# Layer 3's stages beside the next group: four engines on one shared pace, and the same stages with a place of their own for each engine

## The chip, the cores and the metric

One core of a Trainium2 chip runs the whole program. Its engines are TensorE (PE in the profile, with PEld for the loading of weights), VectorE (DVE), ScalarE (ACT), GpSimd (POOL) and SyncE (SP, which here only issues transfers). Each runs its own instructions strictly in the order in which the program gives them, and waits at semaphores for the others. The metric is the device time of one execution in microseconds; lower is better.

## What is computed

Four layers in a row over a batch of 64 sequences of 64 tokens with 256 features, all in float32. Layers 0 to 2 are attentions of x over a context; layer 2 ends in an MLP of 1024 hidden units. Layer 3 is a recurrent block:

```
Mo = softmax(Mn^T Mm) applied to Ml;  x = Wo Mo + x                  # layer 0, channel attention
x = layernorm(gqa(x, ctx) + x)                                       # layer 1, 32 heads of 8
h = rmsnorm(attention(x over [ctx, x]) + x); x = mlp(h) + x          # layer 2, 16 heads of 16
xa = ln(x); sx = shift(xa) - xa                                      # layer 3
xxx = einsum(tanh((xa + sx * maa_x) @ maa_w1), maa_w2)
xk, xw, xv, xr, xg = xa + sx * (maa_stack + xxx)
w = exp(-exp(decay + tanh(xw @ td_w1) @ td_w2)); r, k, v, g = products of xr, xk, xv, silu(xg)
s = k v + w s, over time; out = r (u k v + s)                        # the scan
x1 = x + (groupnorm(out) * g) @ Wo.T
y = x1 + sigmoid(xr2 @ Wfr.T) * (relu(xk2 @ Wfk.T) ** 2 @ Wfv.T)     # xk2, xr2: ln(x1), shifted and mixed
```

## The kernel before

The batch goes in eight groups of eight sequences. `group_block(now, before, after)` is one block of instructions for all engines: it computes layers 0 to 2 of group `now`, layer 3 of group `before`, and near its end loads group `after`. It is called for group 0 (without a layer 3), six times in a loop and once more with both, and at last with a layer 3 alone. So seven blocks hold both kinds of work; they are called turns here. Blocks don't overlap: all engines meet between two of them.

In a turn, layers 0 to 2 are a software pipeline written out by hand. Each engine runs `for i in range(END)` with END = 61. In iteration i layer 0 has its units at i = 0 to 10; layer 1 has its 16 units of scores at i = 14 to 29 (A1 = 14), and layer 2 its 16 at i = 35 to 50 (A2 = 35), each unit going through PE (scores), DVE (`masked`, `largest`), POOL (`subtract`), ACT (`exps`), PE (`turned`) and ACT again. `pair`, `divide`, `project` and `add` follow once for four units; the last `project` of layer 2 (L888) is at i = 58, and what it gives is squared, normalised and turned (`xnT`) by i = 60. Behind the loop PE has the 8 products "u" of the MLP, each with `gelu` on ACT, and two products "y2".

Layer 3 of the group before is a list of stages in order, `STAGES`: 18 from "moments" to "bonus", 19 stages of scans, and 11 from "center" to "ffn v". Every engine calls `layer3(stage)` with its own part of each. In scan stage n POOL makes the products of state n + 1, DVE runs the scan n over time (L1185) and reads the one before (L1197), and PE adds read n - 3 into a bank with one product (L658). When they are called is set by steps: `step()` counts and runs what is due at that count. There are 4 steps ahead of the loop, one in each iteration, one behind each "u" and each "y2", and `rest()` runs what is left.

```python
PACE = {"r u k": 2.2, "shift": 2.2, "maa": 2.2, "gate": 2.4, "shift 2": 2.2,
        "mix 4": 1.0, "r": 1.0, "v": 1.0, "decay": 1.0, "td": 1.2}
due, at = {}, 0.0
for stage in STAGES:
    due.setdefault(int(at), []).append(stage)
    at += PACE.get(stage, 1.0 if stage[0] == "scan" else 1.6)
```

So all engines have a stage in the same iteration: "maa" at i = 3, "mix 0" at 5, "mix 1" at 6, "td" 8, "k" 9, "mix 2" 11, "decay" 12, "v" 13, "mix 3" 14, "mix 4" 16, "r" 17, "g" 18, "r u k" 20, "bonus" 22, the scans one in each iteration from 23 to 41, "center" 42, "variance" 44, "gate" 46, "project" 48, "moments 2" 50, "normalize 2" 51, "turn 2" 53, "shift 2" 54, "ffn k" 57, "ffn r" 58, "ffn v" 60. Nothing of layer 3 is beside the MLP's "u" and "y2". Products of layer 3 go through two banks of their own (ring "late"), those of the other layers through six others.

In an iteration the step comes first on PE, ACT and POOL; on DVE it comes behind `layer0`, `masked` and `largest` and ahead of `normalized`, `divide` and `add`. DVE's `normalize_ahead` for the next group comes behind the "u" steps, and waits for ACT's `deviations_ahead`, which also comes there. SP stores the result of layer 3 (L570) once "ffn v" is done, and waits until it has landed before the block can end. `tables(...)` loads a table of functions on ACT (L928) when another one is set.

## Time and profile before

| | |
|---|---|
| median of 3 runs | 2241.07 us |
| the runs | 2231.89, 2241.07, 2241.25 us |
| the profiled execution, its own time | 2240.95 us |
| its span, first to last instruction | 2239.2 us |
| PE busy | 1800.2 us, 80% |
| DVE busy | 1363.9 us, 61% |
| ACT, POOL busy | 849.3 and 860.1 us, 38% each |
| mean granted clock of TensorE | 0.907 of full speed |
| first "mm" of group 0 (layers 0 to 2 alone) | at 42.4 us |
| the seven turns | from 224.3 to 2092.3 us |
| layer 3 of the last group, alone | from 2092.3 us to the end |

Busy is time in which an engine has an instruction in work. A granted clock of 1.00 is 2.4 GHz, 0.50 is 1.2 GHz; a value between is a stretch with both. Where an engine sat idle, the profile names what ended the idle time. In float32 one matmul of the program shows as two instructions of PE.

### The profile page before, as it was taken

To read this page: it belongs to the slowest core of one execution; us is meant where nothing else is said; L and a number is where in the kernel's file an instruction comes from. 1 tells how busy PE (TensorE), PEld (TensorE's weight loads), DVE (VectorE), ACT (ScalarE), POOL (GpSimd) and SP (SyncE) were. 2 spreads that over 40 slices of the span, in tenths; PEclk is the share of its full clock that TensorE was granted. 3 is DMA by queue.
4 is the path that set the end of the run, shared out by engine and by line. 5 is a ranking of instruction groups with operands and counts; after the bars stand their busy time and mean duration, and the time that the engine had idled before them with its cause. 6 is when DMAs were issued, how large, how long until landed. Compare 5 with 4: busy or idle time off the path is not lost. (4 is left out here: it accounts for less than half of the span.)

```text
span 2239.2 us, 37086 instructions
## 1 busy us (share of the span) xinstructions
PE 1800.2 (80%) x13613; PEld 1098.1 (49%) x13613; DVE 1363.9 (61%) x2332; ACT 849.3 (38%) x1680; POOL 860.1 (38%) x905
## 2 busy tenths in 40 slices
PE   3888887888788787887888878788887888788765
PEld 2565444654356444554445634465444654456413
DVE  3652568635886368753687446873578645875283
ACT  1443432533425333353333533253432543425202
POOL 3531257302672037511384114830257303752060
PEclk9999998999899898898988989899988999889967
DMA  5000011010210102010020101201011010200030
GB/s 157 1 1 25 7 39 39 2 41 1 48 30 13 29 1 63 15 35 7 15 63 1 34 8 25 53 2 41 1 39 39 2 39 1 63 15 11 1 77 10
DMA packets 73611, 61.24 MB, mean 27 GB/s; under 512 B 38960, under 2 KB 56512, under 8 KB 73408
## 3 DMA queue, kind: packets, MB, share of 16 engines
q1 hardware_dynamic: 49600, 41.70, 8.9%
q10 hardware_dynamic: 23264, 16.85, 2.6%
q8 instruction: 122, 2.00, 0.4%
q14 instruction: 81, 0.66, 0.1%
q0 software_dynamic: 544, 0.03, 0.0%
HBM read 20.28 MB, written 4.19 MB: 11 GB/s over the span
## 5 line engine op out<-in xcount | busy, mean ns | idle before, releaser
L1508 POOL TENSOR_TENSOR soft_ring<-soft_ring,seg_max 128x512 f32<-128x512 f32 x256 | 324.2, 1274 | 471.7 <-DVE seg_max L1349 470.9
L1056 ACT ACTIVATE soft_ring<-soft_ring 128x512 f32<-128x512 f32 x256 | 160.8, 628 | 399.3 <-POOL soft_ring L1508 391.6
L658 PE MATMUL bank<-late,pick 128*128 128x512 f32 x256 | 176.4, 779 | 97.4 <-DVE late L1197 97.1
L1343 DVE SCALAR_TENSOR_TENSOR soft_ring<-bank,mask 128x512 f32<-128x512 f32 x256 | 164.4, 683 | 108.2 <-PE bank L716 100.4
L1470 POOL TENSOR_TENSOR late<-late 128x520 f32<-128x520 f32 x128 | 188.7, 1474 | 64.8 <-DMA late<-late 50.1
L1185 DVE TENSOR_TENSOR_SCAN late<-late 128x520 f32<-128x520 f32 x128 | 188.3, 1471 | 19.2 <-POOL late L1472 13.7
L857 PEld LDWEIGHTS bank<-ident,soft_ring 128*128 128x128 f32 x1024 | 126.5, 151 | 122.8 <-issue 97.8
L857 PE MATMUL bank<-ident,soft_ring 128*128 128x128 f32 x1024 | 170.0, 298 | 19.8 <-ACTq L1067 14.0
L1516 POOL TENSOR_SCALAR soft_ring<-soft_ring,rden 128x256 f32<-128x256 f32 x64 | 59.1, 924 | 312.4 <-DVE rden L1310 312.4
L716 PE MATMUL bank<-early 64*128 64x512 f32 (+1 forms) x512 | 128.2, 603 | 58.6 <-ACTq L1049 55.2
L1349 DVE TENSOR_REDUCE seg_max<-soft_ring 128x8 f32<-128x512 f32 (+1 forms) x256 | 169.3, 676 | 8.9 <-DVE early L1406 1.9
L581 PE MATMUL bank<-late,maa 128*128 128x512 f32 (+1 forms) x224 | 127.3, 686 | 23.4 <-DVEq L1177 19.3
L928 ACT ACT_TABLE_LOAD x55 | 70.6, 1283 | 157.2 <-issue 100.8
L1197 DVE TENSOR_TENSOR late<-late 128x512 f32<-128x512 f32 x128 | 122.9, 960 | 0.3 <-PE bank L658 0.3
L658 PEld LDWEIGHTS bank<-late,pick 128*128 128x128 f32 x256 | 50.3, 233 | 143.8 <-DVE late L1197 99.6
L581 PE MATMUL bank<-early,w 128*128 128x512 f32 x256 | 114.7, 607 | 7.4 <-ACT early L1104 7.4
L913 PE MATMUL bank<-w,early 128*128 128x256 f32 x512 | 111.8, 379 | 0.0
L716 PEld LDWEIGHTS bank<-early 64*128 64x128 f32 x512 | 50.3, 218 | 118.8 <-issue 117.2
L913 PEld LDWEIGHTS bank<-w,early 128*128 128x128 f32 x512 | 97.3, 190 | 16.6 <-issue 3.8
L943 ACT ACTIVATE early<-bank,vec 128x512 f32<-128x512 f32 x96 | 66.0, 687 | 102.9 <-PE bank L581 99.8
L1046 ACT ACTIVATE soft_ring<-bank,nmax 128x256 f32<-128x256 f32 x128 | 59.4, 469 | 113.5 <-DVE nmax L1306 109.7
L943 ACT ACTIVATE late<-bank 128x512 f32<-128x512 f32 (+2 forms) x104 | 61.8, 594 | 99.7 <-PE bank L581 97.8
(242 smaller groups left out, 3430.1 us busy)
## 6 DMA issues: line engine op xcount, KB each, us to landing
late<-late SPq DMA_DIRECT2D x128, 260.0 KB, 3.0
c<-in_ctx ACTq DMA_DIRECT2D x8, 512.0 KB, 4.3
x<-in_x ACTq DMA_DIRECT2D x8, 512.0 KB, 5.9
out_x<-late SPq DMA_DIRECT2D x8, 512.0 KB, 5.0
mask<-in_mask_Bx1xSxS_ff ACTq DMA_DIRECT2D x16, 128.0 KB, 4.6
w<-in_L_xattn_mlp_w ACTq DMA_DIRECT2D x2, 1024.0 KB
mask<-in_mask_BxS_ik SPq DMA_DIRECT2D x8, 256.0 KB, 4.1
wkv<-in_L_xattn_kv_w ACTq DMA_DIRECT2D x1, 512.0 KB
```

The lines of the kernel that those rows point to most:

```text
L581: ins = mm(t[0:lhsT_cols(lhsT), 0:cols], lhsT, rhs, start=n == 0, stop=n == len(terms) - 1)
L658: mm(t[:, :], pick[:, j, :], rs[:, j % 2, :], start=j == 0, stop=j == HS - 1).then_inc(full if j == HS - 1 else sig("rs_used"), 1)
L716: ins = mm(t[:, width * n:width * n + width], lhsT, rhs, start=True, stop=True)
L857: ins = tr(t[:, 128 * n:128 * n + 128], soft[:, u % SOFT, 128 * n:128 * n + 128], ident[:, :])
L913: ins = mm(t[:, E * (p % 2):E * (p % 2) + E], gT[:, k, 128 * p:128 * p + 128], w2[:, k, :], start=k == 0, stop=k == HID // 128 - 1)
L943: link(af(dst, src(t), func, **kw))
L1056: af(soft[:, u % SOFT, :], soft[:, u % SOFT, :], ACT.Exp).then_inc(sig("exp"), 1)
L1185: nc.vector.tensor_tensor_scan(sj[:, n % 2, :], wP[:, k, :, :].rearrange("p b t -> p (b t)"), aj[:, n % 2, :], 0.0, ALU.mult, ALU.add).the ...
L1343: stt(out=cuts(u, soft[:, u % SOFT, :]), in0=cuts(u, t[:, :]), scalar=HD1 ** -0.5 if u < UNITS else 1.0 / HD2, in1=mask.unsqueeze(1).broad ...
L1349: nc.vector.tensor_reduce(seg_max[:, u % SOFT, 0:KVH if u < UNITS else 4], cuts(u, soft[:, u % SOFT, :]), X, ALU.max).then_inc(sig("max"), 1)
L1470: tt(aj[:, n % 2, :], kP[:, k, :, :].rearrange("p b t -> p (b t)"), vj[:, n % 3, :], ALU.mult).then_inc(sig("kv_done"), 1)
L1508: tt(s, s, seg_max[:, u % SOFT, 0:segs].unsqueeze(2).broadcast_to([128, segs, 512 // segs]), ALU.subtract).then_inc(sig("sub"), 1)
```

## The change

In place of `PACE` each stage gets four places, one for each engine, in the order PE, ACT, DVE, POOL, and the steps become half iterations: each engine has a second `step()` in every iteration. On PE it lies behind `turned`, on ACT behind layer 0's part and ahead of `between`, on DVE behind `add`, on POOL behind `subtract`. So place 4 + 2i is the first step of iteration i (written "i a" below), 5 + 2i the second ("i b"); 126 to 133 are the steps behind the eight "u", 134 that behind the first "y2". The order of stages on each engine, the instructions of each stage and their waits stay as they are. The diff, with its context cut:

```diff
--- before.py
+++ after.py
@@ -504,14 +504,49 @@
                 "mix 4": 1.0, "r": 1.0, "v": 1.0, "decay": 1.0, "td": 1.2}
-        due, at = {}, 0.0
+        PLACES = {
+            "moments": (0, 2, 0, 6),
+            "normalize": (11, 2, 6, 6),
+            "turn": (11, 11, 10, 6),
+            "shift": (11, 26, 15, 6),
+            "maa": (21, 27, 16, 6),
+            "mix 0": (25, 32, 25, 8),
+            "mix 1": (29, 32, 27, 16),
+            "td": (30, 32, 30, 17),
+            "k": (30, 32, 30, 19),
+            "mix 2": (30, 32, 31, 21),
+            "decay": (33, 32, 31, 21),
+            "v": (37, 34, 35, 21),
+            "mix 3": (37, 40, 36, 27),
+            "mix 4": (43, 40, 40, 32),
+            "r": (45, 43, 41, 43),
+            "g": (45, 44, 43, 43),
+            "r u k": (45, 45, 46, 53),
+            "bonus": (50, 52, 55, 55),
+            "center": (123, 123, 123, 127),
+            "variance": (123, 123, 123, 133),
+            "gate": (123, 123, 123, 133),
+            "project": (127, 127, 126, 133),
+            "moments 2": (130, 128, 126, 133),
+            "normalize 2": (130, 129, 132, 133),
+            "turn 2": (132, 130, 133, 133),
+            "shift 2": (133, 130, 133, 133),
+            "ffn k": (134, 133, 133, 133),
+            "ffn r": (134, 133, 133, 133),
+            "ffn v": (134, 133, 134, 133),
+        }
+        SCAN_PLACES = (
+            (50, 52, 64, 56), (50, 61, 65, 64), (61, 62, 68, 64), (69, 68, 69, 65), (70, 75, 70, 66),
+            (72, 81, 70, 66), (80, 85, 85, 70), (82, 100, 85, 82), (86, 100, 89, 94), (92, 107, 98, 102),
+            (103, 111, 105, 105), (103, 112, 107, 105), (110, 112, 107, 106), (110, 112, 107, 106), (111, 112, 109, 117),
+            (111, 112, 112, 117), (121, 123, 117, 123), (121, 123, 120, 123), (123, 123, 122, 126),
+        )
+        due = {}
         for stage in STAGES:
-            due.setdefault(int(at), []).append(stage)
-            at += PACE.get(stage, 1.0 if stage[0] == "scan" else 1.6)
-
-
-
-
+            spots = SCAN_PLACES[stage[1]] if stage[0] == "scan" else PLACES[stage]
+            for eng, at in zip(("PE", "ACT", "DVE", "POOL"), spots):
+                due.setdefault((eng, at), []).append(stage)
+        LAST = max(at for _, at in due)
 
@@ -534,17 +569,17 @@
 
-            def beside(layer3):
+            def beside(layer3, eng):
 
                 count = [0]
 
                 def step():
-                    for stage in due.get(count[0], []) if before is not None else []:
+                    for stage in due.get((eng, count[0]), []) if before is not None else []:
                         layer3(stage)
                     count[0] += 1
 
                 def rest():
-                    while count[0] <= max(due):
+                    while count[0] <= LAST:
                         step()
@@ -681,7 +716,7 @@
 
-                    step, rest = beside(layer3)
+                    step, rest = beside(layer3, "PE")
                     if now is None:
@@ -894,6 +929,7 @@
                             turned(unit(i - 3))
+                        step()
                         between(i)
@@ -1016,7 +1052,7 @@
 
-                    step, rest = beside(layer3)
+                    step, rest = beside(layer3, "ACT")
 
@@ -1115,6 +1151,7 @@
                             af(s, s, ACT.Identity, scale=rden0[:, i - 1, 1:2]).then_inc(sig("p0b_ready"), 1)
+                        step()
                         between(i)
@@ -1279,7 +1316,7 @@
 
-                    step, rest = beside(layer3)
+                    step, rest = beside(layer3, "DVE")
                     if now is None:
@@ -1438,6 +1475,7 @@
                             add(pair_of(i - 11))
+                        step()
                         between(i)
@@ -1492,7 +1530,7 @@
 
-                    step, rest = beside(layer3)
+                    step, rest = beside(layer3, "POOL")
                     if now is None:
@@ -1516,6 +1554,7 @@
                             subtract(unit(i))
+                        step()
                         for p in range(NP):
```

## Rows read from the trace of the kernel before

**Rows 1.** The page's busy time, of all nine blocks (us, share of the span, instructions).

```profile
PE 1800.2 (80%) x13613; PEld 1098.1 (49%) x13613; DVE 1363.9 (61%) x2332; ACT 849.3 (38%) x1680; POOL 860.1 (38%) x905
```

**Rows 2.** Windows of the third turn: length, busy time, instructions, PE clock, DMA.

```profile
757.93:767.97 10.04, 10.04 (x40) 6.15 (x40) 4.47 (x14) 3.26 (x7) 0.00 (x0) 0.71 0.06 7
767.97:821.59 53.62, 43.69 (x197) 21.22 (x196) 27.64 (x51) 22.29 (x56) 13.15 (x13) 0.94 0.00 1
821.59:857.59 36.00, 29.37 (x205) 14.79 (x204) 24.96 (x39) 14.05 (x24) 17.09 (x16) 0.91 0.15 30
857.59:906.75 49.16, 39.58 (x310) 23.75 (x309) 42.61 (x55) 15.63 (x31) 42.62 (x38) 0.90 0.31 66
906.75:944.18 37.43, 30.95 (x142) 19.71 (x141) 27.14 (x40) 12.54 (x23) 19.84 (x16) 0.82 0.00 1
944.18:988.01 43.83, 36.95 (x694) 29.88 (x694) 29.30 (x55) 25.04 (x50) 10.32 (x12) 0.96 0.01 2
988.01:1027.63 39.62, 31.89 (x116) 21.24 (x115) 12.46 (x36) 13.38 (x23) 3.28 (x13) 0.99 0.22 56
```

**Rows 3.** Windows of group 0's block, without a layer 3, same columns.

```profile
50.35:83.08 32.73, 22.07 (x149) 14.73 (x149) 15.88 (x35) 13.48 (x43) 11.87 (x13) 0.84 0.00 1
83.08:101.08 18.00, 15.20 (x181) 9.38 (x181) 14.79 (x26) 8.82 (x16) 13.38 (x14) 1.00 0.00 1
101.08:131.47 30.39, 27.54 (x289) 19.38 (x288) 14.61 (x30) 14.61 (x30) 11.03 (x13) 0.94 0.01 2
131.47:157.73 26.26, 20.95 (x128) 15.12 (x124) 17.06 (x31) 11.17 (x21) 11.52 (x12) 0.87 0.01 1
157.73:187.42 29.69, 24.71 (x641) 20.25 (x640) 16.69 (x29) 16.46 (x37) 9.60 (x10) 0.94 0.01 3
```

**Rows 4.** Windows of two whole turns, same columns.

```profile
488.30:754.40 266.10, 218.14 (x1696) 133.38 (x1696) 168.84 (x287) 106.13 (x210) 106.09 (x107) 0.93 0.11 25
...
754.40:1024.20 269.80, 222.48 (x1696) 136.72 (x1696) 168.66 (x287) 106.27 (x210) 106.35 (x111) 0.91 0.11 25
```

**Rows 5.** Groups by line: DVE's scans and reads, PE's products L658.

```profile
L658 PE MATMUL bank<-late,pick 128*128 128x512 f32 x256 | 176.4, 779 | 97.4 <-DVE late L1197 97.1
...
L1185 DVE TENSOR_TENSOR_SCAN late<-late 128x520 f32<-128x520 f32 x128 | 188.3, 1471 | 19.2 <-POOL late L1472 13.7
...
L1197 DVE TENSOR_TENSOR late<-late 128x512 f32<-128x512 f32 x128 | 122.9, 960 | 0.3 <-PE bank L658 0.3
```

**Rows 6.** DVE's scan L1185: all 128 (shortest, median, longest ns); two in the last block.

```profile
L1185 DVE TENSOR_TENSOR_SCAN late<-late x128: 1223/1241/2305, 321.5 to 2187.4; 128x520 f32<-128x520 f32 x128
...
2156.39 2.14 DVE L1185 TENSOR_TENSOR_SCAN late<-late 128x520 f32<-128x520 f32 x1
...
2159.21 2.14 DVE L1185 TENSOR_TENSOR_SCAN late<-late 128x520 f32<-128x520 f32 x1
```

**Rows 7.** PE's timeline at the end of the third turn ("u", "y2"): start, us.

```profile
992.12 0.66 PE L762 MATMUL bank<-ident,c 128*128 128x128 f32 x4 [0.69 <-DVE c L1386]
993.70 14.00 PE L581 MATMUL bank<-early,w 128*128 128x512 f32 x32 [0.93 <-ACT early L1104]
1007.54 13.98 PE L913 MATMUL bank<-w,early 128*128 128x256 f32 x64
```

**Rows 8.** Timeline of the last block, layer 3 alone, from "center" to the end.

```profile
2191.67 1.02 PE L581 MATMUL bank<-late,center 128*128 128x512 f32 x2
...
2198.62 1.15 ACT L1000 ACTIVATE late<-late 128x512 f32<-128x512 f32 x2 [0.20 <-ACT late L943]
...
2203.33 5.78 PE L597 MATMUL bank<-t_Wo,late 128*128 128x256 f32 x16 [6.65 <-DVE late L1252]
...
2213.89 1.58 PE L589 MATMUL bank<-ident,late 128*128 128x128 f32 x8 [4.79 <-DVE late L1166]
...
2234.24 0.69 DVE L1279 SCALAR_TENSOR_TENSOR late<-late 128x512 f32<-128x512 f32 x1
```

**Rows 9.** DMA issues of the result: count, KB each, us to landing.

```profile
out_x<-late SPq DMA_DIRECT2D x8, 512.0 KB, 5.0
```

**Rows 10.** ACT's table loads, all blocks (shortest, median, longest ns).

```profile
L928 ACT ACT_TABLE_LOAD  x55: 1283/1283/1283, 42.4 to 2227.6; - x55
```

## The prediction

> **What bounds the kernel now.** I read the page's busy shares first: PE is busy for 80% of the span, DVE for 61%, the others for 38% [rows 1]. So PE is the engine to ask, but a fifth of the time it waits. Next the windows: a turn takes 266 to 270 us, and PE is busy in 218 to 222 of them [rows 4]. The third turn, 269.7 us from its first product to that of the next, is my pattern; it splits into seven stretches [rows 2]: the head (10.04 us), i = 0 to 13 (53.62), i = 14 to 23 (36.00), i = 24 to 34 (49.16), i = 35 to 42 (37.43), i = 43 to the last "out" product at i = 58 (43.83), and the rest with "u", "y2" and the meeting of the engines (39.62). Group 0's block is the same code without a layer 3, and its windows of the same iterations are 32.73, 18.00, 30.39, 26.26 and 29.69 us [rows 3]. The difference is what layer 3 costs in each stretch, and the reader should compare it with layer 3's own products. A product of 512 columns and one term takes 14.00 / 16 = 0.875 us [rows 7]; layer 3 has 72 such terms and two flips of 8 transposes of about 1.0 us each (from 0.66 us for a half, [rows 7]), 65 us in a turn.
>
> By the old places that is 21 us in i = 0 to 13, for 20.9 us more time: no loss. In i = 24 to 34 it is 10 scan products, 8.8 us, for 18.8 us more: here DVE is busy for 42.61 of 49.16 us [rows 2], against 14.61 of 30.39 without a layer 3 [rows 3]. In this stretch DVE sets the pace, not PE: one scan in each iteration, on top of its own work on the scores, and PE's idle time before the scan products (97.4 us in all) ends with DVE's read [rows 5]. In i = 35 to 42 it is 7.0 us for 11.2, in i = 14 to 23 10.5 us for 18.0. At the other end, the last stretch has DVE busy for 12.46 of 39.62 us, ACT for 13.38, and PE without a gap for 28 us of "u" and "y2" [rows 2, 7].
>
> **The change part by part.** No instruction is added or removed but for table loads (below), and a step emits none, so the half steps are free in themselves. Group 0's block has no layer 3, and the last block runs the stages in the same order: both stay. What changes is the seven turns, and I cost one by the seven stretches: time without layer 3, plus layer 3's products that now lie there, plus or minus what waits.
>
> *Head.* The flips go from here to 3b: 10.04 - 1.0 = 9.0 us.
>
> *i = 0 to 13.* A flip and 16 terms ("maa", "mix 0" to "mix 2", "td", "k"), 15.0 us, most of it from 8b on. Layer 0's own gaps (32.73 - 22.07 = 10.7 us, [rows 3]) lie mostly ahead of that, so little is filled: 32.7 + 15.0 = 47.7. DVE still normalises and shifts among layer 0's short waits, and ACT drains the flips; I add 2.3 for it: 50. Filling a quarter of the gaps gives 45; no gain at all is 53.6.
>
> *i = 14 to 23.* 20 terms instead of 12, 17.5 us: 18.0 + 17.5 = 35.5, 36 with a small wait. From below 15.20 us of own products and 17.5: 33. From above, the old loss of 7.5 us on top: 43. ACT takes "v" at 15a, "r" at 19b, while PE gives them at 16b and 20b: the `exps` behind them wait, and PE's `turned` comes three iterations later, which I take as enough cover.
>
> *i = 24 to 34.* Scan products fall from 10 to 3 (2.6 us). DVE gets 14.61 + 1.5 for the bonus (two operations, an estimate) + 6 scans of 1.47 and 5 reads of 0.96 [rows 5] = 29.7 us; PE 30.39 + 2.6 = 33.0. The scans at 30a and 30b stand ahead of `normalized`, for which PE waits: +2, so 35. Bounds 32 and 38.
>
> *i = 35 to 42.* Three scan products in place of six and "center"; DVE 17.06 + 3 x 2.43 = 24.4 us. 26.26 + 2.6 = 29. POOL at 39a waits for the scan at DVE's 40b with `subtract` of two units behind it; they have three iterations, as above. Bounds 26 (both engines' busy time and a little) and 33 (the old loss again).
>
> *i = 43 to "out".* Nine scan products, and on DVE seven scans, eight reads and a `heads` of 0.7, six of these stages between 50b and 54a. Side by side with POOL's products a scan takes 2.14 us and the next starts 2.82 us later; the shortest of all takes 1.22 [rows 6]. In a turn the mean pair is 1.47 + 0.96 = 2.43 [rows 5]. For the bunched stages I take the last block's pace, since it too has scan behind scan: DVE 16.69 + 2.4 + 6 x 2.82 + 0.7 + 0.7 = 37.4 us, above PE's 24.71 + 7.9 = 32.6. So DVE bounds it: 38.5 with a wait. Bounds 35 (pairs at 2.43) and 43.8. The Trainium skill ("SBUF — State Buffer", Who interferes with whom) has it that a DVE instruction with two inputs in SBUF and a GpSimd one that reads SBUF keep each other out, which speaks against bunching; by it the stretch is 38.5, by the turn's mean 36.2, 16 us apart over seven turns, and the rows of the last block agree with it.
>
> *From "out" on*, with T its end (988.01). Five terms come first (the last scan product, "center", "variance", 4.4 us). On ACT "variance" stands ahead of the drain of `xnT`: from the start of "center" to ACT's last Exp is 8.1 us in the last block, 1.28 of it a table load [rows 8, 10] that isn't needed here. So "u" begins at T + 9.3 (now T + 5.7, [rows 7]). Then PE has "u" and "y2", 14.0 + 14.0, and "project", "turn 2" and three ffn products, 15.0 us. Does the chain keep up? "center" to "project" takes 11.7 us, "project" to the second flip 10.6, the flip to the end 21.0 [rows 8]. "project" is due at T + 12.8 by PE (after u0 and u1), by the chain at T + 11.4. The flip is behind u6, T + 25; by the chain T + 24.3, with one table load more. So it is just in time, and I add 1.2 us: PE ends at T + 53.5. ACT holds the drains of u5 to u7 until the flip, but four banks cover that. ACT's tables: "moments 2" between the drains of "u" takes one load away from `gelu` and, since the function needs its table, one back: 1.28 us each [rows 10], inside the chain above. Last, the store. DVE's "ffn v" now stands behind `normalize_ahead`, which waits for ACT behind "ffn r": I estimate its end at T + 52, and the result lands 5.0 us after the issue [rows 9], T + 57.2, while PE and DVE would be done at T + 54: 3.3 us exposed, where before it was hidden by "u" and "y2". With the 6.1 us from PE's end to the next product (39.62 - 33.5, [rows 2, 7]): 62.9. Bounds 58 (store hidden, "u" sooner) and 82 (below).
>
> The sum: 9 + 50 + 36 + 35 + 29 + 38.5 + 62.9 = 260.4 us in place of 269.7, 9.3 us less. Seven turns: 65 us. 2240.95 - 65 = 2176 us; the profiled run is at the median of the runs, so this stands for the median too.
>
> **The rivals.**
>
> *More gain.* The lower bounds make 9 + 45 + 33 + 32 + 26 + 35 + 58 = 238, 31.7 us less in a turn, 2019 us. For it: PE's busy time needs no more than that, and two of the seven stretches run at a granted clock of 0.71 and 0.82 behind idle time [rows 2], so fewer gaps give clock back; a turn at 0.93 has 4.3 us less PE time than one at 0.91 [rows 4]. Against it: layer 0 alone has 10.7 us of gaps. Half way is 2097.
>
> *Given back.* The savings in i = 24 to 42 (22 us) meet the upper bounds of i = 14 to 23 (+7) and of i = 35 to 42 (+4): within 0.5%, about what a measurement of this kernel can tell from no change, 2241 us.
>
> *The tail is paid in full.* Layer 3's last part moves from slack to the one stretch where PE had none. Each engine works strictly in order: if "project" at u1 or the flip at u6 comes late, PE stands with ready "u" behind it. If nothing overlaps, T + 1.0 + 43.3 ("center" to the end, [rows 8]) + 28.0 = T + 72.3, 18.8 us more than I count: a turn of 279.2, 2307 us. The point from which it decides is half of that, 9.3 us. For it: the two dates agree within 1 us, and a late one is never made good. Against it: the last block's chain was taken at its own slow clock of PE ("project" 5.78 us), so it has slack.
>
> **How the numbers follow.** Forecast 0.53 (2130 to 2229), more gain 0.22 (below 2130), given back 0.10, tail 0.15. Predicted: 2176. Faster by over 0.5%: 0.75; within: 0.10; slower: 0.15. The range leaves out the top of the tail case (0.12) and the far end of the gain (0.06): 2080 to 2260; the forecast's own is 2130 to 2229.
>
> **What would show it.** Right: the stretch of i = 24 to 34 near 35 us with DVE busy for some 30; scans at 2.1 us behind i = 50; in the last stretch "u" broken up by layer 3 without gaps over 1 us, 63 us to the next head; the store landing last. PE's wait for L1197 well under 97 us. Wrong: gaps ahead of "project" (DVE L1252) or of the second flip (L1166), scores or `turned` waiting for `exps` held behind "v" or "r" on ACT, or a PE clock well away from 0.91 to 0.93.

## The result, and the profile after

The changed kernel takes 2095.86 us (median of 4 runs, 2094.68 to 2098.45), the one before 2240.73 beside it: ratio 0.9364, interval [0.9338, 0.9389], 6.4% faster. The forecast said 2176. The direction is right and 2095.9 lies in the range, but the gain is 145 us where 65 were forecast; it is the size of the rival "more gain" half way (2097). All times here are of executions in the faster of two states; one of four of spread, 2232.40 us, was in the slower one and is left out. Functions of layer 3 lie 35 to 38 lines further down in the profile after: the products L658 are L693, the scan L1185 is L1222, the read L1197 is L1234, the table load L928 is L964.

The page's busy times of the kernel after, to be held against [rows 1], and of its groups those that answer to [rows 5] (PE's products of the read, DVE's scans):

```profile
PE 1747.7 (83%) x13613; PEld 1080.1 (52%) x13613; DVE 1386.1 (66%) x2332; ACT 856.2 (41%) x1687; POOL 826.5 (39%) x905
...
L1222 DVE TENSOR_TENSOR_SCAN late<-late 128x520 f32<-128x520 f32 x128 | 219.8, 1717 | 15.3 <-DVE early L1401 4.4
L693 PE MATMUL bank<-late,pick 128*128 128x512 f32 x256 | 169.8, 760 | 35.4 <-DVE late L1234 34.8
...
out_x<-late SPq DMA_DIRECT2D x8, 512.0 KB, 2.9
```

PE has the same 13613 instructions and is busy for 52.5 us less (1800.2 before). The span is 143.9 us shorter (2239.2 - 2095.3), so 91.4 us of the gain are idle time of PE that is gone, and 52.5 are instructions that run faster. PE's wait for the read falls from 97.4 us to 35.4. DVE's scan takes 1717 ns in the mean, not 1471.

The windows of the third turn of the kernel after, cut at the same places as [rows 2], and that turn and the next whole, as [rows 4] (length, busy time and instructions of PE, PEld, DVE, ACT, POOL, then PE's clock and DMA):

```profile
716.46:725.55 9.09, 9.09 (x33) 5.26 (x33) 3.36 (x9) 2.56 (x6) 0.00 (x0) 0.69 0.06 7
725.55:769.70 44.15, 37.31 (x190) 21.40 (x189) 26.65 (x52) 19.17 (x51) 14.40 (x22) 0.88 0.00 1
769.70:802.20 32.50, 32.48 (x222) 16.61 (x221) 24.32 (x41) 17.66 (x30) 12.37 (x13) 1.00 0.12 24
802.20:837.11 34.91, 30.58 (x296) 20.45 (x295) 30.13 (x44) 15.08 (x30) 29.55 (x29) 0.95 0.26 56
837.11:865.42 28.31, 23.36 (x131) 15.54 (x131) 24.85 (x37) 10.79 (x21) 16.27 (x14) 0.88 0.09 20
865.42:906.18 40.76, 34.63 (x660) 23.92 (x660) 36.93 (x45) 16.65 (x37) 26.36 (x24) 0.92 0.13 28
906.18:964.70 58.52, 48.22 (x176) 31.36 (x174) 24.79 (x63) 25.50 (x40) 2.06 (x6) 0.97 0.14 38
712.85:961.39 248.54, 215.66 (x1696) 134.54 (x1696) 171.57 (x287) 107.25 (x211) 101.01 (x107) 0.93 0.12 27
...
961.39:1207.18 245.79, 210.32 (x1696) 130.67 (x1696) 172.45 (x287) 107.12 (x211) 101.46 (x107) 0.96 0.12 28
```

The seven stretches add up to 248.2 us, before to 269.7, forecast 260.4. The other turns agree: counted from SyncE's load of `s` in the first of them (224.87 us before, 221.83 after) to that in the last block (2092.35 and 1945.61), the seven turns take 143.7 us less. Three things are to be seen. In i = 14 to 23 PE is busy for 32.48 of 32.50 us at full clock: there is no gap left. In i = 43 to "out" DVE is busy for 36.93 of 40.76. The last stretch is 18.9 us longer than before, and the rest 40.4 us shorter.

The last stretch of the same turn on PE (timeline; start, us, operation, what ended the idle time before it):

```profile
914.43 3.70 PE L616 MATMUL bank<-early,w 128*128 128x512 f32 x8 [2.41 <-ACT early L1140]
917.97 3.62 PE L632 MATMUL bank<-t_Wo,late 128*128 128x256 f32 x16
921.42 8.75 PE L616 MATMUL bank<-early,w 128*128 128x512 f32 x20
930.01 1.04 PE L624 MATMUL bank<-ident,late 128*128 128x128 f32 x8
930.88 1.88 PE L616 MATMUL bank<-early,w 128*128 128x512 f32 x4
932.60 7.07 PE L949 MATMUL bank<-w,early 128*128 128x256 f32 x32
939.51 3.60 PE L616 MATMUL bank<-late,t_Wfk 128*128 128x512 f32 x8
942.94 3.62 PE L632 MATMUL bank<-t_Wfr,late 128*128 128x256 f32 x16
947.19 3.69 PE L632 MATMUL bank<-t_Wfv,late 128*128 128x256 f32 x16 [0.64 <-ACTq L980]
950.72 7.07 PE L949 MATMUL bank<-w,early 128*128 128x256 f32 x32
964.70 1.22 PE L616 MATMUL bank<-early,conv_Wm 128*128 128x512 f32 x1 [6.91 <-issue]
```

"u" (L616) takes "project" (L632), the flip (L624), and "y2" (L949) the three ffn products between its parts, and from 914.43 to 957.79 PE stands only 0.64 us. Both dates on which the tail rival hung, "project" and the flip, are met.

### The profile page after: what moved, and what is told of

It reads as the page before. It is cut to its first block and busy times, and to the rows that moved or that the text cites. A ratio compares the mean times of both kernels' runs of the same rounds, so it can differ in the third digit from the quotient of the medians.

```text
span 2095.3 us, 37093 instructions
## 1 busy us (share of the span) xinstructions
PE 1747.7 (83%) x13613; PEld 1080.1 (52%) x13613; DVE 1386.1 (66%) x2332; ACT 856.2 (41%) x1687; POOL 826.5 (39%) x905
## 5 line engine op out<-in xcount | busy, mean ns | idle before, releaser
L1546 POOL TENSOR_TENSOR soft_ring<-soft_ring,seg_max 128x512 f32<-128x512 f32 x256 | 286.8, 1134 | 338.4 <-DVE seg_max L1386 337.6
L1508 POOL TENSOR_TENSOR late<-late 128x520 f32<-128x520 f32 x128 | 197.9, 1546 | 111.4 <-DVE late L1222 59.0
L1222 DVE TENSOR_TENSOR_SCAN late<-late 128x520 f32<-128x520 f32 x128 | 219.8, 1717 | 15.3 <-DVE early L1401 4.4
L693 PE MATMUL bank<-late,pick 128*128 128x512 f32 x256 | 169.8, 760 | 35.4 <-DVE late L1234 34.8
L892 PEld LDWEIGHTS bank<-ident,soft_ring 128*128 128x128 f32 x1024 | 116.1, 143 | 94.0 <-issue 67.7
L751 PE MATMUL bank<-early 64*128 64x512 f32 (+1 forms) x512 | 118.9, 566 | 48.6 <-ACTq L1085 44.3
L616 PE MATMUL bank<-early,w 128*128 128x512 f32 x256 | 121.1, 625 | 17.8 <-ACT early L1140 17.8
L616 PE MATMUL bank<-late,maa 128*128 128x512 f32 (+1 forms) x224 | 111.1, 618 | 4.7 <-DVE late L1255 3.1
L1234 DVE TENSOR_TENSOR late<-late 128x512 f32<-128x512 f32 x128 | 111.7, 873 | 2.5 <-PE bank L693 2.5
L949 PE MATMUL bank<-w,early 128*128 128x256 f32 x512 | 113.0, 379 | 0.0
L949 PEld LDWEIGHTS bank<-w,early 128*128 128x128 f32 x512 | 97.3, 190 | 16.6 <-issue 3.8
L1213 DVE SCALAR_TENSOR_TENSOR late<-bank,vec,late 128x512 f32<-128x512 f32 x80 | 59.7, 746 | 61.4 <-PE bank L616 57.5
L693 PEld LDWEIGHTS bank<-late,pick 128*128 128x128 f32 x256 | 50.0, 229 | 91.8 <-DVE late L1234 59.3
L1510 POOL COPY late<-s 128x8 f32<-128x8 f32 x128 | 92.8, 725 | 8.1
```

Source lines behind the costliest of these rows:

```text
L616: ins = mm(t[0:lhsT_cols(lhsT), 0:cols], lhsT, rhs, start=n == 0, stop=n == len(terms) - 1)
L693: mm(t[:, :], pick[:, j, :], rs[:, j % 2, :], start=j == 0, stop=j == HS - 1).then_inc(full if j == HS - 1 else sig("rs_used"), 1)
L751: ins = mm(t[:, width * n:width * n + width], lhsT, rhs, start=True, stop=True)
L892: ins = tr(t[:, 128 * n:128 * n + 128], soft[:, u % SOFT, 128 * n:128 * n + 128], ident[:, :])
L949: ins = mm(t[:, E * (p % 2):E * (p % 2) + E], gT[:, k, 128 * p:128 * p + 128], w2[:, k, :], start=k == 0, stop=k == HID // 128 - 1)
L1222: nc.vector.tensor_tensor_scan(sj[:, n % 2, :], wP[:, k, :, :].rearrange("p b t -> p (b t)"), aj[:, n % 2, :], 0.0, ALU.mult, ALU.add).the ...
```

## The experiments

All ratios are to the kernel before, run on the same chip; different versions ran on different chips. The table gives the third turn by the seven stretches of [rows 2], in us, from each run's own windows. The head and i = 0 to 13 differ by some 1 us each between versions with the same code in them (9.1 and 44.2 in the changed kernel, 8.2 and 43.2 in "ahead"), with a granted clock of 0.69 and 0.88 against 0.76 and 0.92: differences of that size in these two columns are not read as effects of a change. In the expectations numbers of stretches are iterations; where one says that a stage stands "at i=16", or "one iteration behind" another, it counts places: place 16 is the first step of iteration 6, half an iteration behind place 15.

| version | ratio | head | 0–13 | 14–23 | 24–34 | 35–42 | 43–out | last |
|---|---|---|---|---|---|---|---|---|
| before | 1 | 10.0 | 53.6 | 36.0 | 49.2 | 37.4 | 43.8 | 39.6 |
| changed | 0.936 | 9.1 | 44.2 | 32.5 | 34.9 | 28.3 | 40.8 | 58.5 |
| f_front | 0.969 | 8.7 | 43.1 | 32.5 | 51.5 | 38.4 | 45.1 | 39.9 |
| f_tail | 1.008 | 9.0 | 53.0 | 34.1 | 50.3 | 35.7 | 29.2 | 58.5 |
| f_front_tail | 0.975 | 7.8 | 42.2 | 32.5 | 51.5 | 36.7 | 29.5 | 58.5 |
| f_scan_tail | 0.975 | 9.2 | 53.1 | 34.1 | 34.3 | 28.3 | 40.8 | 60.7 |
| one_dve | 1.025 | 7.9 | 53.4 | 34.8 | 42.7 | 31.4 | 40.7 | 65.7 |
| act_as_pe | 0.941 | 7.8 | 42.1 | 35.2 | 33.7 | 28.6 | 40.7 | 60.6 |
| pe_as_dve | 1.009 | 7.8 | 52.0 | 38.2 | 37.7 | 28.4 | 40.7 | 65.0 |
| pool_as_dve | 0.952 | 8.1 | 43.2 | 32.5 | 37.1 | 30.6 | 41.3 | 60.7 |
| pe_act_front_dve | 0.985 | 8.0 | 53.4 | 34.8 | 36.8 | 28.3 | 40.7 | 60.3 |
| ahead | 0.929 | 8.2 | 43.2 | 32.5 | 34.9 | 28.3 | 40.7 | 57.7 |
| maa_near | 0.952 | 8.3 | 49.3 | 32.5 | 33.7 | 28.7 | 40.7 | 60.0 |
| maa_mid | 0.931 | 8.1 | 43.8 | 32.5 | 34.9 | 28.3 | 40.7 | 57.6 |
| wide | 0.941 | 7.9 | 45.8 | 32.5 | 33.7 | 28.7 | 40.7 | 59.4 |
| sooner | 0.983 | 7.9 | 55.5 | 34.2 | 34.9 | 28.3 | 40.7 | 58.0 |
| spread | 0.940 | 8.2 | 43.2 | 32.5 | 34.9 | 28.3 | 43.5 | 58.7 |
| tail_dve | 0.939 | 9.3 | 44.1 | 32.5 | 33.7 | 30.4 | 40.7 | 60.2 |
| ffn_near | 0.948 | 9.3 | 44.1 | 32.5 | 33.6 | 30.4 | 40.7 | 62.9 |
| two_back | 0.972 | 8.4 | 46.3 | 36.6 | 36.9 | 28.3 | 41.1 | 61.5 |

### Which part of the change gives what

The front (18 stages), the scans and the tail (11 stages) were given their new places apart, the rest the old ones. f_front, as a diff to the changed kernel (GpSimd's "r u k" and all of "bonus" stand at 50, ahead of the old first scan):

```diff
-            "r u k": (45, 45, 46, 53),
-            "bonus": (50, 52, 55, 55),
-            "center": (123, 123, 123, 127),
+            "r u k": (45, 45, 46, 50),
+            "bonus": (50, 50, 50, 50),
+            "center": (88, 88, 88, 88),
...
-            (50, 52, 64, 56), (50, 61, 65, 64), (61, 62, 68, 64), (69, 68, 69, 65), (70, 75, 70, 66),
+            (50, 50, 50, 50), (52, 52, 52, 52), (54, 54, 54, 54), (56, 56, 56, 56), (58, 58, 58, 58),
```

> Only the front of layer 3 (the 18 stages from 'moments' to 'bonus') gets its new places; scans and tail stay at the old ones. Theory: what each part of the change does is local and adds up, and layer 3's front products fill the idle time that layers 0 to 2 leave on TensorE in i = 0 to 23, instead of standing on top of it as the prediction had it. Then the stretches of i = 0 to 13 and 14 to 23 become about 44 and 33 us as in the changed kernel (from 53.6 and 36.0), 13 us less in each of seven turns, 91 us in all: 2150 us. Rival: the front gains only because the scans are thinned out behind it and VectorE has room; then with the old scans it stays within 15 us of 2241.

> Only the tail ('center' to 'ffn v') gets its new places, from i = 59 on and beside the MLP; front and scans at the old ones (scans in i = 23 to 41). Theory: the tail's move alone earns nothing. The last stretch grows by 18.9 us as in the changed kernel, while i = 43 to 58 falls from 43.8 to about 31 (29.7 without a layer 3) and i = 35 to 42 by 2: about 4 us more in a turn, 2265 us. Rival: the tail's move is itself the gain, since it fills VectorE's and ScalarE's slack beside the MLP: 2190 us or less.

> Front and tail at the new places, scans at the old ones (i = 23 to 41, one in each iteration). Theory of parts that add up: the front's 91 us less and the tail's 28 us more, 2177 us; i = 24 to 34 stays at 49 us with VectorE busy for some 43. Rival: thinning the scans isn't needed, 2110 us or less.

> Scans and tail at the new places, front at the old ones. Theory: i = 0 to 23 stays at 89.6 us as before, the rest is as in the changed kernel: 2096 + 91 = 2187 us. Rival: the front's new places don't matter by themselves, within 20 us of the changed kernel's 2096.

Measured: 2166.27 us, 0.9685 [0.9645, 0.9725]; 2254.39, 1.0081 [1.0058, 1.0103]; 2179.17, 0.9748 [0.9702, 0.9795]; 2180.98, 0.9745 [0.9704, 0.9786]. The parts nearly add up: front and tail together are within 0.2% of the product of the two ratios (0.9748, 0.9764); scans and tail times front give 0.944 where the changed kernel has 0.936, about as much as the intervals leave open. The front alone came 16 us short of its theory (2150), since i = 24 on took 4.8 us a turn more. The front is worth 3.2%, made in i = 0 to 23 (14.0 us less) and in part given back in i = 24 on. The tail by itself costs 0.8%: i = 43 to "out" gets 15 us shorter and the last stretch 19 us longer. The scans, spread over the room that the tail leaves, are worth 3.4% on top of the tail (1.0081 to 0.9745) and 3.8% on top of both (0.9748 to 0.9364).

### Do the engines need places of their own

The same places, one column for all engines (here "maa" stands for all 48 lines):

```diff
-            "maa": (21, 27, 16, 6),
+            "maa": (16, 16, 16, 16),
```

> All four engines take the places of VectorE's column: the new distribution of the stages in half iterations, but one pace shared by all engines, as in the kernel before. Theory: the gain is where the stages lie (front later, scans thinned to i = 59, tail beside the MLP), not that each engine has its own place, since the waits at semaphores would place them anyway; own places are worth no more than some 3 us in a turn: 2096 to 2117 us. Rival: own places are the gain, because an engine that stops at a stage too soon holds up the attention work behind it: 2170 us or more.

Measured: 2297.97 us, 1.0247 [1.0223, 1.0272]. My theory, that only the spread over the turn matters, fell. With the new spread and one column the kernel is slower than before the change; own places are worth 200 us. Next, one engine at a time:

```diff
-            "maa": (21, 27, 16, 6),
+            "maa": (21, 21, 16, 6),   # act_as_pe: ScalarE on TensorE's column
+            "maa": (16, 27, 16, 6),   # pe_as_dve
+            "maa": (21, 27, 16, 16),  # pool_as_dve
+            "maa": (16, 16, 16, 6),   # pe_act_front_dve: front stages only
```

> The changed kernel, but ScalarE's places are TensorE's. Theory: ScalarE is idle for more than half the time and its exps have three iterations of cover, so it stays within 10 us of the changed kernel's 2096. Rival: in the tail ScalarE's 'moments 2' now stands behind u4's gelu instead of u2's, and its 'turn 2' behind u6's; the second flip comes late, TensorE stands for 2 to 4 us in each turn: 2110 to 2125 us.

> Only TensorE gives up its own places and takes VectorE's column; ScalarE, VectorE and GpSimd keep theirs. The run with all engines on VectorE's column took 276.5 us a turn against 248.5. Theory: the loss is TensorE's. It then comes to the maa products at i=16, one iteration behind the shift that VectorE makes for them at i=15 (the changed kernel has 21), stops there, and ScalarE's and VectorE's attention work stops behind it. It expects i=0 to 13 at about 52 us (44.2 in the changed kernel), i=24 to 34 at 40 or more (34.9), a turn near 268 and a time of 2220 to 2270. Rival: the loss is ScalarE's or the sum of small shifts of all; then this run is within 25 us of the changed kernel's 2096, with i=0 to 13 near 44.

> Only GpSimd gives up its own places and takes VectorE's column. Theory (the loss of the common column comes from TensorE): GpSimd is busy 39% of the span and what it makes is wanted late, so this is within 15 us of 2096, turn 248 to 250. Rival: GpSimd's early front places (its moments and mixes at i=6 to 21 where VectorE has 0 to 36) are what lets layer 3's front run in layer 0's gaps; then i=0 to 13 and i=14 to 23 grow by 3 us or more a turn together and the time is above 2125.

> TensorE and ScalarE take VectorE's places for the front stages alone (moments to bonus, with the first two scan places moved behind them, 50 to 55); the scan stages and the tail keep the changed kernel's places for every engine. Theory (TensorE's and ScalarE's margin behind VectorE in the front is what counts in the first stretches): i=0 to 13 about 52 us (44.2), i=14 to 23 about 34.5 (32.5), i=24 to 34 within 1.5 of 34.9, the rest unchanged, in all +10 a turn, 2165. Rival (the margin is worth nothing in the front, the loss of the common column is made in the scans and the tail): within 15 us of 2096.

Measured: 2109.06 us, 0.9410 [0.9387, 0.9432]; 2257.43, 1.0093 [1.0065, 1.0121]; 2130.05, 0.9520 [0.9495, 0.9545]; 2202.74, 0.9845 [0.9816, 0.9874]. TensorE's own places are worth 161 of the 202 us; i = 0 to 13 grew as expected (52.0), i = 24 to 34 less than expected (37.7, not 40 or more). GpSimd's are worth 34, the rival's size but not in the rival's place: i = 0 to 23 doesn't grow, and the loss is in i = 24 to 42 and the last stretch. ScalarE's cost 13, between the theory (within 10) and the rival (2110 and more). But act_as_pe also has ScalarE's three ffn places at 134, which by themselves gain 13 us ("ahead", below); against "ahead" the rest of ScalarE's places are worth 26. TensorE and ScalarE in the front alone lose 107 us where 70 were expected.

### The distance to the producer

On "ahead" (below), one place of one engine is changed: TensorE's "maa" from 21 to 16 or to 18, with VectorE's shift, which makes its input, at 15.

```diff
-            "maa": (21, 27, 16, 6),
+            "maa": (16, 27, 16, 6),   # maa_near
+            "maa": (18, 27, 16, 6),   # maa_mid
```

> One number differs from the version that took 2083: TensorE comes to the maa products at i=16, one iteration behind VectorE's shift, and not at 21. Theory: this distance carries most of the first stretch's gain; i=0 to 13 takes 49 to 53 us where that version has 43.2, the products wait 3 us or more for VectorE and then run in over 5 us at the lower clock where they take 3.72, i=14 to 23 stays within 1 us of 32.5, and the time is 2125 to 2150. Rival: the first stretch needs all the front stages in their own places, one number does little, and the time is below 2105.

> The same one number at 18, three iterations behind the shift. VectorE's four shift operations came 0.7 us apart and ended some 3 us after TensorE had asked in the version at 16 of the common column; two iterations more are some 6 us in this stretch. Theory: by then the input is there, the wait is gone and the time is within 10 us of 2083. Rival (every iteration of distance counts): half of what one iteration behind costs, 2100 or more.

Measured: 2130.16 us, 0.9516 [0.9492, 0.9539]; 2085.14, 0.9310 [0.9287, 0.9332]. One number of 192 is worth 47 us; maa_mid is 2 us from "ahead", within the interval. TensorE's timeline in maa_near:

```profile
745.58 1.09 PE L775 MATMUL bank<-early 128*64 128x256 f32 x8
750.17 6.45 PE L616 MATMUL bank<-late,maa 128*128 128x512 f32 x8 [3.49 <-DVE late L1255]
756.55 1.14 PE L751 MATMUL bank<-early 64*128 64x256 f32 x8
```

VectorE at the same time (the last two of the shift's four operations):

```profile
748.64 0.68 DVE L1254 TENSOR_TENSOR late<-late 128x512 f32<-128x512 f32 x1
749.36 0.75 DVE L1255 SCALAR_TENSOR_TENSOR late<-late,vec 128x512 f32<-128x512 f32 x1
```

And the windows of maa_near before and at the products, then the same of "ahead" (a fence each):

```profile
745.58:750.17 4.59, 1.09 (x9) 0.51 (x9) 4.14 (x7) 2.04 (x6) 0.92 (x1) 0.85 0.00 0
750.17:756.55 6.38, 6.38 (x9) 1.65 (x9) 0.00 (x0) 0.00 (x0) 0.00 (x0) 0.58 0.00 0
```

```profile
733.00:738.50 5.50, 3.90 (x31) 2.72 (x29) 5.04 (x11) 2.18 (x8) 1.24 (x2) 1.00 0.00 1
738.50:742.15 3.65, 3.65 (x11) 0.94 (x9) 1.92 (x5) 3.41 (x8) 1.53 (x2) 1.00 0.00 0
```

The reader sees two costs of one early place. TensorE comes 3.49 us too soon, while VectorE still makes the shift. The products then run with the clock granted at 0.58, mostly the lower of its two levels, and take 6.38 us; at 1.00 the same eight take 3.65. While they run, VectorE, ScalarE and GpSimd are busy for 0.00 us: the scores that all three want (L751) stand behind them on TensorE, and the next begin at 756.55. That is 3.49 + 2.73 = 6.2 us, and the stretch is 6.1 longer. The kernel before has the second cost too, its products 5.86 us long behind a wait of 5.40 for ScalarE. With three places of distance (maa_mid) TensorE waits 0.77 us, the products take 3.82, and the stretch is 0.6 us longer.

The other side: VectorE's shift two places sooner, and, with the earlier front on three engines, much sooner:

```diff
-            "shift": (11, 26, 15, 6),
-            "maa": (21, 27, 16, 6),
+            "shift": (11, 26, 13, 6),   # wide
+            "maa": (21, 27, 14, 6),
...
+            "turn": (7, 7, 7, 6),       # sooner
+            "shift": (7, 8, 11, 6),
+            "maa": (16, 20, 12, 6),
+            "mix 0": (21, 26, 20, 8),
```

> The distance made larger from the other side: VectorE makes the shift at 13 and takes maa at 14 (15 and 16 in the version of 2083), TensorE stays at 21. Theory: the input was there in time already, more distance gives nothing, and the time is within 10 us of 2083. Rival (VectorE's earlier operations stop for ScalarE or TensorE and hold its softmax work behind them, as in the run with all front places earlier): i=0 to 13 grows by 3 us or more and the time is above 2100.

> On top of the version with ScalarE's three ffn places behind the deviations (2083), layer 3's front comes 1 to 6 iterations sooner on three engines: TensorE's turn and shift at 7, maa 16, mix 0 at 21, mix 1 at 25; ScalarE's turn 7, maa 20, mixes from 26; VectorE's turn 7, shift 11, maa 12, mix 0 at 20. In the changed kernel i=0 to 13 takes 44.2 us with 37.3 of TensorE busy, so 6.8 us of gaps are open there, and i=14 to 23 has none (32.48 of 32.50). Theory (front work fills gaps where its input is there): i=0 to 13 keeps its length with more TensorE busy, i=14 to 23 falls by 2 to 3, in all 2 to 3 us a turn, 2062 to 2072. Rival (front work so near behind its producer stops the engine's own queue, as on the common column): i=0 to 13 grows by 3 us or more and the time is 2095 or above.

Measured: 2107.36 us, 0.9409 [0.9387, 0.9431]; 2196.61, 0.9830 [0.9803, 0.9857]. Both are slower than "ahead", and both times my theory lost to the rival, although i = 0 to 13 of "wide" grew by 2.6 us and not by 3. In "wide" TensorE waits 3.85 us for a softmax of layer 0 where "ahead" has 1.00:

```profile
744.77 2.08 PE L751 MATMUL bank<-early 64*128 64x256 f32 x8 [3.85 <-ACTq L1085]
```

because VectorE makes the shift first, and the row maximum (L1343) that ScalarE needs stands behind it (VectorE in "wide"):

```profile
740.00 0.69 DVE L1254 TENSOR_TENSOR late<-late 128x512 f32<-128x512 f32 x1 [0.22 <-DVE early L1353]
...
742.11 0.75 DVE L1255 SCALAR_TENSOR_TENSOR late<-late,vec 128x512 f32<-128x512 f32 x1
742.78 0.68 DVE L1343 TENSOR_REDUCE nmax<-bank 128x2 f32<-128x512 f32 x1
```

In "sooner" the flip stands one place behind "normalize" and waits (TensorE), and there are more like it: TensorE waits 4.00 us for ScalarE, and VectorE 8.03 for TensorE:

```profile
757.68 1.38 PE L624 MATMUL bank<-ident,late 128*128 128x128 f32 x8 [3.78 <-DVE late L1203]
```

So neither attempt fills the 6.8 us of gaps that are left in layer 0's stretch. That no other places would fill them isn't shown.

### The tail, and two places more

```diff
-            "ffn k": (134, 133, 133, 133),
-            "ffn r": (134, 133, 133, 133),
-            "ffn v": (134, 133, 134, 133),
+            "ffn k": (134, 134, 133, 133),   # ahead; ffn_near has 133 first here,
+            "ffn r": (134, 134, 133, 133),   # and here
+            "ffn v": (134, 134, 134, 133),
```

> The changed kernel, but ScalarE's 'ffn k' and 'ffn r' come one step later, behind deviations_ahead, so that VectorE's normalize_ahead no longer waits for them and 'ffn v' and the store come sooner. In the changed kernel the store is issued 1.3 us before VectorE's last addition starts and lands 0.9 us behind its end. Theory of the prediction (the store is exposed, by less than it said): 0.5 to 1 us less in a turn, 3 to 7 us in all, ratio 0.997. Rival: the end of the block is set by TensorE's y2 and the meeting of the engines; no difference.

Measured: 2083.19 us, 0.9294 [0.9273, 0.9314], 13 us faster than the changed kernel and, with maa_mid, the fastest version here. Of this 3 to 7 us were expected. ScalarE no longer holds `deviations_ahead` behind "ffn v", so VectorE's `normalize_ahead` and the store come sooner: the last stretch is 0.8 us shorter, 6 us over seven turns. The other half is in the head and i = 0 to 13 (0.9 and 1.0 us in this turn), whose code is the same and whose granted clock is higher; why it is isn't shown.

> On the version of 2083 only TensorE's four places in the tail go to VectorE's: project 126 (127), moments 2 126 (130), normalize 2 132 (130), turn 2 133 (132). Theory: the 6.8 us that the last stretch lost with TensorE on VectorE's column (65.0 against 58.2) is made by these; the stretch takes 63 us or more where that version has 57.7, the rest stands, and the time is 2118 to 2135. Rival: it comes from layers 0 to 2's side or from the scans before, and the stretch stays below 60 us, the time below 2095.

> On the version of 2083, TensorE's ffn k and ffn r go from place 134 (behind the first y2) to 133, where VectorE has the shift that they read. Theory: the ffn k products wait about 4 us for VectorE and then take over 6 us in place of 3.60, so the last stretch is 63.5 to 65 us (57.7) and the time 2122 to 2135. Rival (the tail's loss on the common column was in places 126 to 133 and in ScalarE's gelu): the wait is under 1 us and the time below 2100.

> The version with TensorE on VectorE's column (2257, first stretch 52.0, last 65.0), with three of its 48 places given back: maa at 21, ffn k and ffn r at 134. Theory: the two distances are most of what that column costs; i=0 to 13 falls to 43 to 46 us, the last stretch to 58 to 61, and the time to 2150 to 2175. Rival (the loss is spread over the other 45 places, the mixes and the scans): the time stays above 2210.

tail_dve has "project" at 126, "moments 2" at 126, "normalize 2" at 132 and "turn 2" at 133 on TensorE; two_back is pe_as_dve with "maa" at 21 and "ffn k", "ffn r" at 134. Measured: 2102.50 us, 0.9393 [0.9369, 0.9417]; 2122.48, 0.9475 [0.9454, 0.9497]; 2176.83, 0.9724 [0.9708, 0.9740]. The four places make 2.5 us in the last stretch, not the 6 I gave them, and the time is between theory and rival. The ffn products at the same place as VectorE's second shift make 5.2, with the signature of maa_near, if less of it than expected: a wait of 2.48 us where I gave it about 4, and 5.40 us of products where I gave them over 6 (TensorE in ffn_near; with the changed kernel's places they take 3.60):

```profile
943.38 5.40 PE L616 MATMUL bank<-late,t_Wfk 128*128 128x512 f32 x8 [2.48 <-DVE late L1307]
```

Three places given back to pe_as_dve return 81 of its 161 us, just outside what I expected (2150 to 2175). Of the 11.0 us that its turn is still longer than the changed kernel's, 4.1 lie in i = 14 to 23, 2.2 in i = 0 to 13, 2.0 in i = 24 to 34 and 3.0 in the last stretch; which of the 45 places make them was not tried.

### Scans apart instead of bunched

```diff
-            (72, 81, 70, 66), (80, 85, 85, 70), (82, 100, 85, 82), (86, 100, 89, 94), (92, 107, 98, 102),
-            (103, 111, 105, 105), (103, 112, 107, 105), (110, 112, 107, 106), (110, 112, 107, 106), (111, 112, 109, 117),
+            (72, 81, 70, 66), (80, 85, 85, 70), (82, 100, 85, 82), (86, 100, 89, 94), (92, 107, 96, 96),
+            (97, 111, 98, 99), (99, 112, 101, 102), (102, 112, 104, 105), (105, 112, 107, 108), (108, 112, 110, 111),
```

> The changed kernel with scan stages 9 to 17 laid out evenly, one in each one and a half iterations on VectorE, TensorE and GpSimd, instead of six of them bunched between i = 50 and 54. Theory of the prediction: bunched scans run against GpSimd's products at 2.82 us for a pair of scan and read and bound i = 43 to 58; laid out evenly they cost 2.4, 2 to 3 us less in a turn: 2075 to 2085 us, and the stretch falls from 40.8 to 38 us. Rival: VectorE has too little idle time in this stretch wherever the scans lie, or the scans then hold up the scores: 2096 us or more.

Measured: 2109.30 us, 0.9397 [0.9362, 0.9432], an interval that overlaps the changed kernel's. The mean scan got a little shorter (1663 ns, 1717), but the stretch got longer (43.5 us, 40.8), with DVE busy for 37.18: the bunching isn't what costs there, and the theory is out.

Not tried: all engines on TensorE's, ScalarE's or GpSimd's column, ScalarE alone on VectorE's, and places rounded to whole iterations: in those orders, as I read the program, engines would wait for each other in a circle. What the half iterations as such are worth stays open.

## Why the prediction was right in sign and wrong in size

**What held.** Much of the time is in TensorE's gaps, and costs by stretch can be held against the seven windows. Head 9.09 (9.0). i = 24 to 34: 34.91 us (35) with DVE busy for 30.13 (29.7). i = 35 to 42: 28.31 (29). "u" begins at T + 8.25 (T + 9.3, T = 906.18), the flip is at T + 23.8 (T + 25), PE ends at T + 51.6 (T + 53.5). The tail costs as forecast, in kind: alone it makes the kernel slower.

**The step that failed** is in the terms of i = 0 to 13 and of i = 14 to 23: "time without layer 3, plus layer 3's products". Layer 3's 15.0 and 17.5 us were put on top of 32.7 and 18.0, with 2.3 us and 0.5 us for waits. The stretches took 44.15 (50 forecast) and 32.50 (36). Layer 0's own gap is 10.7 us [rows 3], and 3.6 us of it were filled (47.7 - 44.15); in the second, the gap of 2.8 us [rows 3] was filled whole: 15.20 + 17.5 = 32.7, near my lower bound of 33. TensorE's gaps in i = 0 to 13, first those of group 0 (kernel before, no layer 3), then the changed kernel's:

```profile
54.79 2.08 PE L716 MATMUL bank<-early 64*128 64x256 f32 x8 [3.31 <-ACTq L1049]
60.48 2.08 PE L716 MATMUL bank<-early 64*128 64x256 f32 x8 [2.56 <-ACTq L1049]
```

```profile
729.99 2.08 PE L751 MATMUL bank<-early 64*128 64x256 f32 x8 [3.31 <-ACTq L1085]
735.67 2.08 PE L751 MATMUL bank<-early 64*128 64x256 f32 x8 [0.86 <-ACTq L1085]
745.42 1.09 PE L775 MATMUL bank<-early 128*64 128x256 f32 x8 [1.60 <-DVE early L1353]
```

A fourth wait of group 0, 1.00 us, stays as it is. That most of the gaps lie ahead of place 21 was right: these stay, but for the flip in one of them, and one of 0.38 us grew to the 1.60. That "little is filled" behind them was wrong: group 0 has five further gaps of 0.3 to 1.3 us there, 3.3 in all, and the changed kernel has none from 745.42 on. So layer 3's products filled all that lay beside their new places, and none of them waited. The premise came from reading the kernel before as "21 us for 20.9 us more time: no loss". It had filled next to nothing (53.62 - 43.69 = 9.9 us of gaps are left), and its first eight products of "maa" ran in 5.86 us behind a wait for ScalarE:

```profile
774.51 2.08 PE L716 MATMUL bank<-early 64*128 64x256 f32 x8 [5.40 <-ACTq L1049]
776.52 5.86 PE L581 MATMUL bank<-late,maa 128*128 128x512 f32 x8
```

These two terms are 9.4 us of the 12.2 by which the turn was forecast too long. The experiments say when filling works: a place far enough behind its producer waits little (0.77 us at 18 for a shift at 15) or not at all (21). The forecast took the new places of each engine as neutral ("what waits" was a margin of 0.5 to 2.3 us), and never priced what they prevent: on one column the same spread costs 9.2 us in i = 0 to 13 and 202 us in all.

**The last stretch**, 58.52 against 62.9, is a term mis-sized. The store (L605 at 956.52) lands 2.9 us after its issue, not 5.0. Without a store in the way, SyncE begins the next block 1.91 us after VectorE's last operation ("ahead"), here 2.87 us, so the store's exposure is 1.0 us and not 3.3 (T + 52 and 5.0 us make T + 57.0 and 3.0 by themselves; nothing hangs on the slip). The timeline of the changed kernel, then that of "ahead":

```profile
956.52 0.41 SPq L605 DMA_DIRECT2D out_x<-late  x1
957.83 0.69 DVE L1489 TENSOR_TENSOR x<-bank,xr 128x512 f32<-128x512 f32 x1 [1.48 <-PE bank L949]
961.39 0.38 SPq L590 DMA_DIRECT2D mask<-in_mask_BxS_ik  x1
```

```profile
943.66 0.41 SPq L605 DMA_DIRECT2D out_x<-late  x1
...
948.86 0.69 DVE L1489 TENSOR_TENSOR x<-bank,xr 128x512 f32<-128x512 f32 x1 [5.38 <-PE bank L949]
951.46 0.38 SPq L590 DMA_DIRECT2D mask<-in_mask_BxS_ik  x1
```

"u" and PE's end came 1.1 and 1.9 us sooner as well.

**i = 43 to "out"**, 40.76 against 38.5, was too short. DVE's busy time was as forecast (36.93, 37.4); the waits were 3.8 us and not 1.1. The mean scan rose to 1717 ns from 1471. A scan is longer when GpSimd's product for a later state (L1508) runs beside it. By the two engines' timelines, of the third turn's 16 scans those without it take 1.22 to 1.24 us (but for one of 1.87, beside another operation of GpSimd's), those with 1.03 to 1.05 us of it beside them 2.13 to 2.14, and one with 1.13 us only 1.72. Beside GpSimd's small copy (L1510) alone a scan keeps its 1.23:

```profile
818.79 1.23 DVE L1222 TENSOR_TENSOR_SCAN late<-late 128x520 f32<-128x520 f32 x1
890.35 1.23 DVE L1222 TENSOR_TENSOR_SCAN late<-late 128x520 f32<-128x520 f32 x1
892.27 2.13 DVE L1222 TENSOR_TENSOR_SCAN late<-late 128x520 f32<-128x520 f32 x1
```

```profile
818.78 1.23 POOL L1510 COPY late<-s 128x8 f32<-128x8 f32 x1
891.73 1.58 POOL L1508 TENSOR_TENSOR late<-late 128x520 f32<-128x520 f32 x1 [1.45 <-DVE late L1222]
```

With the product's rows agrees what the Trainium skill ("SBUF — State Buffer", Who interferes with whom) says, that a VectorE instruction with two inputs in SBUF and a GpSimd one that reads SBUF get in each other's way. Putting the scans apart gained nothing (spread).

**The clock** had no term. PE's same instructions take 52.5 us less in the run, more than a third of the gain, and the rival "more gain" named this with too little weight [rows 4]. That a wait lowers the clock of what follows is seen at single places (maa_near). Of the 52.5 us, 16.2 are in one group, layer 3's products that read `maa` or its mixes (before, then after):

```profile
L581 PE MATMUL bank<-late,maa 128*128 128x512 f32 (+1 forms) x224 | 127.3, 686 | 23.4 <-DVEq L1177 19.3 <-DVE late L1218 3.1 <-ACTq L945 0.8
```

```profile
L616 PE MATMUL bank<-late,maa 128*128 128x512 f32 (+1 forms) x224 | 111.1, 618 | 4.7 <-DVE late L1255 3.1
```

The mean granted clock of the run rose only from 0.907 to 0.923; by that ratio alone 1800.2 us would become 1769, an estimate, so the mean doesn't account for all 52.5 us, and no run separates them.

With the measured stretches the sum closes: 12.2 us less in each turn is 85 over seven, and 2176 - 85 = 2091, 0.2% from the median. The first block came out 3.0 us shorter and the last 2.9 longer, so "both stay" held.

**Luck.** That the rival's half way point, 2097, is the measured time is in part chance. Its lower bounds were reached or nearly so in i = 0 to 23 and the last stretch (44.15 for 45, 32.50 for 33, 58.52 for 58), while i = 24 to 42 came out at the forecast and i = 43 to "out" well above its bound of 35.

## What to carry to other kernels

Where engines run strictly in order, place each engine's share of a side job far enough behind its producer's that the producer is done: half an iteration behind cost 47 us in one stage, one and a half cost 2 us, within the interval. Find the distance in the trace, from the wait in front of the consumer. Here moving the consumer back was free, and moving the producer ahead cost 24 us ("wide"), because the producer's engine has main work behind it too. When the main work has gaps on the bounding engine, go through them one by one: those behind the point where side work is ready were filled whole here (3.3 and 2.8 us), those ahead of it stayed.

## What the hardware showed that I had not expected

- A store of 512 KB landed in 2.9 us where before it took 5.0 [rows 9] (medians of eight); before, it was issued beside the loads of the next group. No run takes these loads away alone.
- The same eight products take 3.65 us at a granted clock of 1.00 and 6.38 at 0.58, right behind 3.5 us in which TensorE stood. So the engine that came too early paid its wait nearly twice.
- The same scan takes 1.23 us by itself and 2.13 with GpSimd's product beside it, from the rows shown above.
- ScalarE has 62 table loads in place of 55 [rows 10]: one of 1.28 us in each of the seven turns, at the drain of the MLP's products behind "moments 2".
